# One register load of eight offsets in place of eight loads, on the sync engine of a graph network layer

## What is computed

```python
h = jnp.maximum(_layernorm(x, axis=-1), 0.0)
edge_input = jnp.concatenate([h[src], h[dst], edge_attr_32, coordination[src], coordination[dst]], axis=-1)
messages = jax.nn.silu(edge_input @ mW1 + mb1) @ mW2 + mb2
aggregated = jax.ops.segment_sum(messages, dst, num_segments=n_nodes)
u = jax.nn.silu(jnp.concatenate([h, aggregated, coordination], axis=-1) @ uW1 + ub1)
out = x + _layernorm(h + u @ uW2 + ub2, gamma, beta)
```

## Time and profile before

| | us |
|---|---|
| median of 3 runs | 687.73 |
| runs, lowest and highest | 686.38, 688.04 |
| the profiled execution | 688.41 |
| span of the profiled execution | 686.5 |
| PE busy | 622.7 |
| DVE busy | 620.1 |
| ACT busy | 546.5 |
| POOL busy | 498.4 |

### The profile page before, as it was taken

How to read it: one execution, slowest core, us unless ns; L and a number is a source line. 1 busy time by engine, 2 the same in 40 slices (tenths; PEclk the granted TensorE clock), 3 DMA queues, 4 the chain that set the end, 5 groups by cost and what they waited for, 6 DMA issues and landing times.

```text
span 686.5 us, 17715 instructions
## 1 busy us (share of the span) xinstructions
PE 622.7 (91%) x3756; PEld 447.0 (65%) x3756; DVE 620.1 (90%) x2905; ACT 546.5 (80%) x1181; POOL 498.4 (73%) x447
## 2 busy tenths in 40 slices
PE   2879999999999999999999999999999999999872
PEld 1346776676676676776776776766766767767652
DVE  4666989999999999999999999999999999998787
ACT  1469998898898888888898898888888898898620
POOL 7777878887787887887777777788787888873100
PEclk9999999999999999999999999999999999999997
DMA  6545566676666666666676676666676676674332
GB/s 147 184 121 141 160 189 182 183 194 182 175 198 183 181 193 181 184 192 178 189 198 170 187 199 171 185 199 172 185 203 168 185 205 176 181 213 132 92 83 96
DMA packets 91988, 119.07 MB, mean 173 GB/s; under 512 B 20250, under 2 KB 65493, under 8 KB 91944
## 3 DMA queue, kind: packets, MB, share of 16 engines
q1 hardware_dynamic: 64436, 43.37, 22.7%
q0 software_dynamic: 12752, 26.57, 20.5%
q10 hardware_dynamic: 14756, 48.66, 18.4%
HBM read 79.63 MB, written 38.70 MB: 172 GB/s over the span
## 4 chain that ended last, share of the span: by engine, by line
DVE 33%; POOL 19%; issue 19%; PE 10%; DMA 10%; ACT 4%; SPq 3%; DVEq 1%; POOLq 0%; ACTq 0%
POOL ends_in L447 18%; DMA ends_in<-in_rows,end_idx 9%; DVE y_out L888 9%; DVE stats L921 6%; DVE stats L911 3%; DVE stats L973 3%; DVE centred L858 3%; DVE stats L972 2%; SPq L388 2%; ACT ends_norm L672 2%; SPq L379 1%; PE ps_hid L598 1%; ACT x_norm L672 1%; PE ps_t L569 1%; PE ps_upd L610 1%
## 5 line engine op out<-in xcount | busy, mean ns | idle before, releaser
L447 POOL DMA_INDIRECT ends_in<-in_rows,end_idx x392 | 384.2, 980 | 113.5 <-issue 105.1
L672 ACT ACTIVATE ends_norm<-ends_in,minus,rstd 128x128 f32<-128x128 f32 x392 | 160.4, 482 | 6.2 <-DVE minus L1025 5.1
L672 ACT ACTIVATE x_norm<-x_in,minus,rstd 128x128 f32<-128x128 f32 x392 | 155.5, 482 | 0.0
L598 PEld LDWEIGHTS ps_hid<-match,msg_in 113*128 113x128 f32 x784 | 99.3, 191 | 83.2 <-DVE match L874 57.2
L470 POOL TENSOR_TENSOR x_beta<-x_in,beta_row 128x1024 f32<-128x1024 f32 x47 | 111.2, 2366 | 36.0 <-DVE y_out L888 20.2
L888 DVE SCALAR_TENSOR_TENSOR y_out<-centred,rstd,x_beta 128x128 f32<-128x128 f32 x392 | 127.9, 335 | 2.7 <-issue 0.4
L598 PE MATMUL ps_hid<-match,msg_in 113*128 113x128 f32 x784 | 108.0, 280 | 21.0 <-DVE match L874 20.8
L766 ACT ACTIVATE hidden_n<-ps_hid,node_bias 128x512 f32<-128x512 f32 x98 | 67.2, 686 | 63.1 <-PE ps_hid L598 59.1
L921 DVE BATCH_NORM_STATS2 stats<-ps_upd 128x6 f32<-128x128 f32 x392 | 109.5, 288 | 3.5 <-issue 2.6
L610 PE MATMUL ps_upd<-w_out,hidden_n 128*128 128x128 f32 x784 | 105.2, 278 | 7.9 <-DVE centred L858 7.9
L858 DVE SCALAR_TENSOR_TENSOR centred<-ps_upd,y_mean,gamma_row 128x128 f32<-128x128 f32 x392 | 107.3, 338 | 0.0
(11 more groups left out here) (92 smaller groups left out, 782.0 us busy)
## 6 DMA issues: line engine op xcount, KB each, us to landing
out<-y_out ACTq DMA_DIRECT2D x48, 512.0 KB, 2.8
x_in<-in_x_steps ACTq DMA_DIRECT2D x44, 512.0 KB, 4.2
msg_in<-msgs SPq DMA_DIRECT2D x392, 56.4 KB
msgs<-msg SPq DMA_DIRECT2D x49, 258.0 KB, 2.7
ends_in<-in_rows,end_idx POOLq DMA_INDIRECT x392
feat_t<-in_attr SPq DMA_DIRECT2D x25, 128.0 KB
x_in<-in_x_steps SPq DMA_DIRECT2D x5, 512.0 KB, 3.6
feat_t<-coords SPq DMA_DIRECT2D x98, 2.0 KB
```

The costliest lines, as they stand in the source:

```text
L447: nc.gpsimd.indirect_dma_start(out=dst, out_offset=None, in_=rows, in_offset=bass.IndirectOffsetOnAxis(ap=end_idx[s.slot // 2][:, s.slot % ...
L598: last = nc.tensor.matmul(ps_hid[:, cols(j)], msg_in[k.half][0:WINDOW + 1, j, 0:H], match[k.half][0:WINDOW + 1, j, :], start=False, stop=j ...
L672: return nc.scalar.activation(dst, source, function, bias=minus[was][:, c:c + 1], scale=rstd[was][:, c:c + 1])
```

## The change

In each iteration with nodes, SP's eight loads of one register each are replaced by one load instruction that names eight registers and a range of eight integers of `first_edge`. The registers are named by a counter, so that each iteration written out has its own. The windows use them as before, and nothing else is touched; the lines behind the change move down by three (on SP) or five. Here `soon` is the node step whose windows are loaded and `N_TILES` is 8.

```diff
+            names = count()
...
-                    return [sp.value_load(first_edge[0:1, bass.ds(N_TILES * soon.n + j, 1)]) for j in range(N_TILES)]
+                    regs = [sp.alloc_register(f"first{next(names)}") for j in range(N_TILES)]
+                    sp.load(regs, first_edge[0:1, bass.ds(N_TILES * soon.n, N_TILES)])
+                    return [sp.snap(r, donate=True, min_val=0, max_val=EDGES_PAD) for r in regs]
```

More of the change, by code:

```diff
@@ L1 @@
 from contextlib import ExitStack
+from itertools import count
 import concourse.bass as bass
```

## The result

The changed kernel took 682.19 us, the median of 10 runs (679.84 to 685.12), against 687.41 us for the kernel before on the same chip (10 runs). The ratio, taken from the single runs and not from the two medians, is 0.9935, with a 95% interval of 0.9915 to 0.9954: 4.5 us less, between 3.2 and 5.8. By the medians alone it is 5.2 us less. The forecast was 3.65 us less. Its profiled execution took 685.12 us, with a span of 683.3.

What follows compares the result with a forecast made beforehand. The kernel was taken as bound by POOL's gathers, their landing and DVE's work on them. Gains of 1.55 + 1.1 + 1.0 = 3.65 us off the median 687.73 gave 684.1 us, range 681.5 to 688.2.

Steps and rivals of the forecast that it cites:

- the three places: Only at A, B and C is SP on the chain: store of msg, offset loads, windows, landing that DVE awaits.
- A: Ahead of the loop, store at 82.61 us: first window 1.55 us sooner, gain 1.55 us, bounds 0 and 1.7.
- B: At the end, store at 619.90 us: first window 1.57 us sooner, gain 1.11 us, which is DVE's wait.
- C: At the end, store at 646.02 us: landing 3.3 us, first window 1.0 us sooner, gain 1.0 us.
- The load's price: One load of eight registers at A takes 0.78 us, where the eight loads take 3.5 us.
- The landing takes the loads' place: With short loads SP waits for the store's landing, median 2.7 us; first window follows 0.3 us after landing.
- Rival 3: More than the sum: A grows to 1.7 us, shorter landings in the loop add 2.7 us; 681.4 us, chance 0.10.
- The loop: From 120 to 600 us SP is not on the chain; windows are there before they are wanted, so gain nothing.
- Rival 2: Earlier windows lengthen the gathers' landings in the loop, 0.35 us each, 6.3 us in all: 690.4 us, chance 0.11.
- Rival 1: Nothing gained: new load takes about 3.5 us like the eight, 687.7 us; chance 0.27, including A given back.
- A given back: Rival 1's other form: cheap load, but A swallowed by the other chain, sum 2.1 us, 685.6 us; within chance 0.27.

Runs made afterwards that it cites:

- f1: Single load of eight registers only behind the loop, eight loads elsewhere, against the kernel before: 684.14 us against 686.69, ratio 0.9962.
- f3: Single load only ahead of the loop (iterations 3 to 8), eight loads elsewhere, against the kernel before: 684.52 us against 686.69, ratio 0.998.
- f2: Single load only inside the loop (iterations 9 to 44), eight loads elsewhere, against the kernel before: 686.70 us against 686.69, ratio 0.9994.
- g3: Changed kernel using one register of the load of eight, plus seven single loads behind it; against the kernel before 687.51 us against 687.16, ratio 1.0002.
- g1: The changed kernel again, for a second profile, against the kernel before: 682.78 us against 687.16, ratio 0.994.
- g4: Changed kernel with two loads of four registers in place of one of eight; 682.62 us, ratio 0.9947 to the kernel before.
- g2: Changed kernel with two loads of eight registers, windows using half of each; 684.17 us, ratio 0.9955 to the kernel before.

## Why the prediction was right

**The bound, and the three places.** SP was on the chain at A, B and C alone, and the gain is there and nowhere else: f1 holds most of it, f3 the rest (though its interval just includes none), f2 has none, and g3, which gives SP's time back, loses it all. Right.

**The load's price.** I took 0.78 us at A. The median of all 49 is 0.79, but that agreement is luck: at A, B and C the load took 1.04, 1.09 and 1.02 us, so this term was some 0.3 us too low where it counts. It cost nothing, because the load still ended 1.8 us behind the store's start, ahead of the landing.

**The landing takes the loads' place.** Right, and it is why loads that end 2.4 to 2.6 us sooner gave less than that at all three places. The wait appeared in 48 iterations. g3 shows from the other side that it was SP's time.

**A.** Forecast 1.55 us, measured 1.1 in the marks and 1.4 by f3's ratio. This term came out smaller. The first window came 2.6 us behind the store in f3 and g1 and 3.1 in after, where 3.0 was forecast. The stall in the windows' issue at A went away as well: from the first issue's start to the last one's end it was 6.5 us before, and 3.9 to 4.4 in after, f3, g1 and g4. (In f1, with eight loads there, it was 4.9, so it isn't the loads' alone.) Rival 3 gave A 1.7 us for that case, and A still gave 1.1: part was taken back by what is late next, as the text allowed, but which wait took it is not shown.

**B.** Forecast 1.1, measured 1.0. In after both halves of `match` 45 start at once:

```profile
628.05 1.59 DVE L879 SCALAR_TENSOR_TENSOR match<-iota_sb,const_sb,msg_in 112x512 f32<-112x512 f32 x2
```

The 1.11 us of idle time of the earlier trace rows is gone, and no more could be had there, since DVE came to it without a pause.

**C.** Forecast 1.0, measured 1.9. This is the term that was mis-sized most, and with it the sum (3.65 forecast, 4.0 by the marks, 4.5 by the ratio). C was 0.9 us too low and A 0.45 too high, so part of the error cancels. I took the landing of that one store, 3.3 us, from the profile of before. In the profiles with short loads it was 2.4 (after), 2.8 (f1), 2.5 (g1) and 2.4 (g4). The page's median of 49 stores, 2.7, would have given 1.6. A single value of a thing that scatters should have stood as a bound and the median in the sum. The old form did not make it long either: with eight or more loads at C the same store landed in 2.7 (f2), 2.4 (f3) and 2.5 us (g3). So 3.3 belongs to that one execution; what made it long there is open.

**The loop.** Forecast 0, measured 0.0006 of the time in f2, within its interval. Rival 2, windows that lengthen the gathers' landing, had its chance there and shows nothing: f2 isn't slower. The sign that the prediction named for it, gathers on the chain that take 3.7 us or more to land, is missing too: from 120 to 600 their median was 3.5 us before, 3.5 after and 3.4 in f2. In the waits of after, 120 to 600, against the earlier trace rows:

```profile
DVE stats L977 <- DMA ends_in<-in_rows,end_idx: 7.8, 20, 1.2
...
POOL x_beta L475 <- DVE match L879: 12.3, 18, 0.9
```

The same two waits, 8.6 and 11.9 us before, set the period.

**The rivals.** Rival 1 (dear load) is refuted by the load's line, though g3 is what it would have looked like, and its other form, A given back, by the marks of A. Rival 3 asked for shorter landings in the loop; the shortest median of these is that of f1, 3.3 us, which has eight loads there, so they don't follow the loads. The Trainium skill ("Runtime: NRT & Kernel Launch", "Instruction fetch mechanics") puts a register load at about 200 ns per register, which made an estimate of 1.6 us for eight. That page tells of registers loaded from HBM (its section "Terms"), and here they come from SBUF. The measurement decides: medians of 0.79 us as the first load and 0.53 us as the second, so 66 to 99 ns per register, and 0.8 to 1.6 us for eight at A, B and C.

**The range** of 681.5 to 688.2 holds 682.19. It is near its lower end and 1.9 us below the forecast of 684.1: the sum was 0.9 us too small by the ratio, before itself was 0.3 us faster in the ten runs beside it, and the rest is scatter between runs.

## What to carry to other kernels

An engine that only issues transfers can hold the end in a few iterations and be idle in all the others: find these in the chain in order of time, and cost a shorter stretch there by the wait that stands right behind it, not by what was cut. Here some 2.5 us less of register loads was worth 1 to 2 us at each of three places and nothing at the 46 others. Once the landing of a transfer is the bound, look for issue work that doesn't depend on it and can go ahead, and count first how much of the landing is already used, with the durations at that place and not with medians over the whole span.

## What the runs showed of the hardware

A register load from SBUF on SP costs by the trip more than by the register: as medians, behind another load 0.27 us for one register, 0.30 us for four (g4) and 0.53 us for eight (g2). The first one behind transfers costs about 0.26 us more, 0.57 us for four and 0.79 us for eight. That four cost hardly more than one, and eight as much as two times four, looks like a trip per four registers; this is a guess from three counts, and others I did not measure.

The place matters as much. Outside the loop a load of eight took 1.0 to 1.1 us in most iterations. In the profile of before, the third and fourth loads at A took 0.67 and 0.53 us where their neighbours took 0.26 and 0.27 (the chain, 82 to 88):

```profile
84.50 0.67 SPq L379
85.20 0.53 SPq L379
```

They ran 1.9 to 3.1 us behind the store's start, and in the same stretch g2's second load took 1.21 us at A and 1.22 at C. So loads were slow there while the store was landing. That the store is the cause is not shown.
